# Listing each slot's token in PSUM instead of scattering rows to the experts

## The reference, cut to what matters

```python
x = x + gnn(xn, edge_index, ...) + mix(xn, ...)
...
logits = layernorm(x) @ gate_w + gate_b
probs = softmax(logits); idx = argmax(probs); prb = probs[idx]
pos = (cumsum(one_hot, axis=0) * one_hot).sum(-1) - 1     # place within the expert
kept = pos < C                                            # C = 1954
buf[idx, pos] = layernorm(x)                              # dropped where pos >= C
y = relu(buf @ w1[e] + b1[e]) @ w2[e] + b2[e]
x = x + y[idx, pos] * (prb * kept)
```

## Time and profile before

| what | us |
|---|---|
| median of 3 runs (lowest, highest) | 1644.87 (1641.97, 1651.89) |
| the profiled execution | 1646.12 |
| its span, first to last instruction | 1644.4 |
| PE busy in the span | 1414.5 |
| DVE busy | 1178.4 |
| ACT busy | 766.7 |
| POOL busy | 622.2 |

### The profile page before, as it was taken

The page is one execution under the profiler, slowest core; times in us unless marked ns, Lnnn a source line. Parts: engine busy times, 40 slices in busy tenths (PEclk is TensorE's granted clock), DMA queues, the critical chain, the costliest instruction groups (busy, mean ns, idle before and its releaser), DMA issues. The chain is left out here.

```text
span 1644.4 us, 29280 instructions
## 1 busy us (share of the span) xinstructions
PE 1414.5 (86%) x8633; PEld 1252.5 (76%) x8633; DVE 1178.4 (72%) x3066; ACT 766.7 (47%) x1455; POOL 622.2 (38%) x541
## 2 busy tenths in 40 slices
PE   6999999985858766777724999999999999999995
PEld 5999999974646555565524999999999999999995
DVE  5888888864777767777753676677767686767764
ACT  3455555531112111111114676766767676766762
POOL 1111111117787887888860122222122222222213
PEclk8999999996686787777766999999999999999998
DMA  3555555552445554555425212121121312131100
GB/s 108 127 122 120 119 122 130 127 161 59 105 106 123 125 114 107 113 119 121 104 67 127 76 40 72 44 77 47 41 87 50 94 42 77 48 100 50 26 14 18
DMA packets 122639, 145.22 MB, mean 88 GB/s; under 512 B 61546, under 2 KB 97390, under 8 KB 122469
## 3 DMA queue, kind: packets, MB, share of 16 engines
q1 hardware_dynamic: 70897, 89.24, 21.5%
q0 software_dynamic: 51696, 55.42, 14.0%
HBM read 76.42 MB, written 73.36 MB: 91 GB/s over the span
## 5 line engine op out<-in xcount | busy, mean ns | idle before, releaser
L1256 POOL DMA_INDIRECT out<-o_sb,tok_i x128 | 177.7, 1388 | 604.9 <-issue 604.9
L1454 DVE TENSOR_TENSOR h_lo<-hf,h_hi 128x496 fp32r<-128x496 f32 x256 | 172.8, 675 | 214.4 <-PE psY L1515 88.5
L1515 PE MATMUL psY<-w_hi,h_hi 128*124 128x256 f32 x1024 | 290.1, 283 | 7.6 <-DVE w_lo L1368 7.6
L1515 PE MATMUL psY<-w_hi,h_lo 128*124 128x256 f32 x1024 | 287.8, 281 | 0.0
L1515 PE MATMUL psY<-w_lo,h_hi 128*124 128x256 f32 x1024 | 287.2, 280 | 0.0
L1329 ACT ACTIVATE h_hi<-psH,b_sb 128x496 fp32r<-128x496 f32 x256 | 172.7, 674 | 230.0 <-PE psH L1538 219.5
L1515 PEld LDWEIGHTS psY<-w_hi,h_hi 128*124 128x124 f32 x1024 | 189.3, 185 | 16.0 <-issue 8.0
L1515 PEld LDWEIGHTS psY<-w_lo,h_hi 128*124 128x124 f32 x1024 | 189.5, 185 | 8.9
L1515 PEld LDWEIGHTS psY<-w_hi,h_lo 128*124 128x124 f32 x1024 | 189.7, 185 | 0.0
L1071 PE MATMUL psB<-inv_den,spread_at 128*128 128x125 f32 x400 | 84.0, 393 | 114.0 <-DVE inv_den L856 114.0
L1331 ACT ACTIVATE hf<-psH,b_sb 128x496 f32<-128x496 f32 x256 | 170.9, 668 | 0.0
(11 more groups left out here) (217 smaller groups left out, 3035.1 us busy)
## 6 DMA issues: line engine op xcount, KB each, us to landing
x_sb<-in_x SPq DMA_DIRECT2D x50, 448.0 KB
...
out<-o_sb,tok_i POOLq DMA_INDIRECT x128, 4.2
```

What stands on the lines that cost most here:

```text
L1256: pool.indirect_dma_start(out=out, in_=o_sb[:, par, j, :], in_offset=None, out_offset=bass.IndirectOffsetOnAxis(ap=tok_i[:, par, j:j + 1], ...
L1454: nc.vector.tensor_tensor(h_lo[:, f % 4, :], hf[:, f % 4, :], h_hi[:, f % 4, :].bitcast(F32), ALU.subtract).then_inc(s_hlo_ready, 1)
L1515: ins = nc.tensor.matmul(psY[par][j // 2][0:T3, (j % 2) * D:(j % 2 + 1) * D], hh[:, f % 4, j * T3:(j + 1) * T3], w[:, f, :], start=f == 0 ...
```

## The change

The buffer `expert_rows` goes, with the clears that fill it in stage 1, the row scatter of stage 2 and the loads of stage 3. Instead a list says which token each slot holds. A slot is written as a block and a row of it (slot = 124 block + row, NB = 128 blocks). DVE works out both in `place`; ACT makes, for each of a step's four tokens a partition, a one-hot of the row (124 wide) and one of the block (128 wide), the latter once with the token's index plus one and once with the probability's factor in place of the 1. It makes them by |i - row| and a Relu. PE multiplies the two (`listed`), and the sums of all 25 steps stay in one PSUM bank `psP`. After the last step DVE turns it into `row_at` (slots that stayed zero get an index out of bounds) and `prob`.

In stage 3 POOL gathers each tile's rows from the output, where stage 2 stored them, by four indirect DMAs with `row_at`, and scatters the results with it too. Empty slots are skipped by the gather, so DVE clears the four buffers first. The order on DVE changes: att_scores of step s+1 now stands ahead of `place(s)`. `positions` moves from a bank of its own to a part of `psD`, and `q_ksum` and `positions` get a wait for it.

```diff
-                def clear(g):
-                    pool.dma_start(groups[bass.ds(g, 1), :, :, :].rearrange("a p j w -> (a p) j w"),
-                                   empty[:, :].rearrange("p (a w) -> p a w", a=1).broadcast_to([P, J, RW]))\
-                        .then_inc(s_empty_out, 16)
...
                 pool.wait_ge(s_mhalf_set, 1)
-                for s in range(3):
+                rstd_of(0)
+                with pool.Fori(1, NS) as s:
                     rstd_of(s)
-                    clear(s)
-                with pool.Fori(3, NS) as s:
-                    rstd_of(s)
-                    clear(s)
-                with pool.Fori(NS, E * ROWS // (P * J)) as s:
-                    clear(s)
...
-                nc.gpsimd.iota(token[:, :], [[1, J]], base=0, channel_multiplier=J,
+                nc.gpsimd.iota(val[:, 0, :], [[1, J]], base=1 - TS, channel_multiplier=J,
                                allow_small_or_imprecise_dtypes=True)
-                nc.gpsimd.memset(xd[:, :, :, :], 0.0)
+                nc.gpsimd.iota(upto[:, 0:T3], [[1, T3]], base=0, channel_multiplier=0,
+                               allow_small_or_imprecise_dtypes=True)
+                nc.gpsimd.iota(upto[:, T3:T3 + NB], [[1, NB]], base=0, channel_multiplier=0,
+                               allow_small_or_imprecise_dtypes=True)
...
-                def scatter(s, par):
-                    pool.wait_ge(s_slots_ready, s + 1)
-                    passed(pool, s_pool_passed)
-                    for j in range(J):
-                        pool.indirect_dma_start(out=rows, in_=xd[:, par, j, :], in_offset=None,
-                                                out_offset=bass.IndirectOffsetOnAxis(ap=slots[:, par, j:j + 1], axis=0),
-                                                bounds_check=E * ROWS - 1, oob_is_err=False).then_inc(scat[par], 16)
...
                     if ahead == 2:
                         pool.wait_ge(s_pr, NPR * s + 1)
                         gather(s + 2, par, h + 2)
-                    scatter(s, par)
...
+                def one_hots(s):
+                    act.wait_ge(s_place, NPLACE * (s + 1))
+                    act.wait_ge(s_perm_mm, s)
+                    act.wait_ge(s_at_ready, 3 * J * s)
+                    act.activation(nval[:, :, :], val[:, :, :], ACT.Copy, scale=-1.0).then_inc(s_away, 1)
+                    passed(act, s_act_passed)
+                    for j in range(J):
+                        act.activation(away[:, j, 0:T3], upto[:, 0:T3], ACT.Abs, bias=row[:, j:j + 1], scale=-1.0)\
+                           .then_inc(s_away, 1)
+                    for j in range(J):
+                        act.activation(away[:, j, T3:T3 + NB], upto[:, T3:T3 + NB], ACT.Abs, bias=blk[:, j:j + 1],
+                                       scale=-1.0).then_inc(s_away, 1)
+                    act.wait_ge(s_away, NAWAY * (s + 1))
+                    passed(act, s_act_passed)
+                    for j in range(J):
+                        act.activation(at_row[:, j, :], away[:, j, 0:T3], ACT.Relu, bias=1.0, scale=-1.0)\
+                           .then_inc(s_at_ready, 1)
+                        for n in range(2):
+                            act.activation(at_block[:, j, n, :], away[:, j, T3:T3 + NB], ACT.Relu, bias=val[:, n, j:j + 1],
+                                           scale=nval[:, n, j:j + 1]).then_inc(s_at_ready, 1)
                 def step(s, par, h, ahead):
                     root(s)
                     logit_exp(s)
                     if ahead > 0:
                         att_exp(s + 1)
+                    one_hots(s)
...
-                    nc.vector.tensor_scalar(xd[:, par, :, D + 1], token[:, :], 0.0, None, ALU.add)
...
-                    nc.vector.tensor_scalar(token[:, :], token[:, :], float(TS), None, ALU.add)
...
-                def place(s, par):
+                def place(s):
                     dve.wait_ge(s_l_exp, s + 1)
                     nc.vector.tensor_reduce(lsum[:, :], lex[:, :, :], axis=AX.X, op=ALU.add).then_inc(s_route, 1)
                     dve.wait_ge(s_pos_mm, s + 1)
                     nc.vector.tensor_tensor(pos[:, :, :], cum[:, 0:J, :],
-                                            psC[0:T, 0:E].rearrange("p (a e) -> p a e", a=1).broadcast_to([T, J, E]),
+                                            psD[0:T, 128:128 + E].rearrange("p (a e) -> p a e", a=1).broadcast_to([T, J, E]),
                                             ALU.add).then_inc(s_route, 1)
                     nc.vector.tensor_tensor(seen[:, :], seen[:, :], cum[:, J, :], ALU.add)
                     dve.wait_ge(s_route, NROUTE * s + 9)
                     nc.vector.tensor_tensor(picked[:, :, :], pos[:, :, :], oh[:, :, :], ALU.mult).then_inc(s_route, 1)
-                    dve.wait_ge(s_route, NROUTE * s + 8)
-                    nc.vector.reciprocal(xd[:, par, :, D], lsum[:, :])
                     dve.wait_ge(s_route, NROUTE * s + 10)
                     nc.vector.tensor_reduce(slotf[:, :], picked[:, :, :], axis=AX.X, op=ALU.add).then_inc(s_route, 1)
+                    dve.wait_ge(s_at_ready, 3 * J * s)
+                    nc.vector.tensor_scalar(val[:, 0, :], val[:, 0, :], float(TS), None, ALU.add).then_inc(s_place, 1)
+                    dve.wait_ge(s_route, NROUTE * s + 8)
+                    nc.vector.reciprocal(val[:, 1, :], lsum[:, :]).then_inc(s_place, 1)
                     dve.wait_ge(s_route, NROUTE * s + 11)
-                    nc.vector.tensor_tensor(over[:, :], slotf[:, :], limit[:, :], ALU.is_ge).then_inc(s_route, 1)
-                    dve.wait_ge(s_route, NROUTE * s + 12)
-                    nc.vector.scalar_tensor_tensor(slots[:, par, :], over[:, :], BIG, slotf[:, :], ALU.mult, ALU.add)\
-                      .then_inc(s_slots_ready, 1)
+                    nc.vector.tensor_tensor(over[:, :], slotf[:, :], limit[:, :], ALU.is_ge).then_inc(s_place, 1)
+                    dve.wait_ge(s_place, NPLACE * s + 3)
+                    nc.vector.scalar_tensor_tensor(slotf[:, :], over[:, :], BIG, slotf[:, :], ALU.mult, ALU.add)\
+                      .then_inc(s_place, 1)
+                    dve.wait_ge(s_place, NPLACE * s + 4)
+                    nc.vector.tensor_scalar(blk[:, :], slotf[:, :], 1.0 / T3, 0.5 / T3 - 0.5, ALU.mult, ALU.add)\
+                      .then_inc(s_place, 1)
+                    dve.wait_ge(s_place, NPLACE * s + 5)
+                    nc.vector.tensor_scalar(blk[:, :], blk[:, :], ROUND, ROUND, ALU.add, ALU.subtract).then_inc(s_place, 1)
+                    dve.wait_ge(s_place, NPLACE * s + 6)
+                    nc.vector.scalar_tensor_tensor(row[:, :], blk[:, :], -float(T3), slotf[:, :], ALU.mult, ALU.add)\
+                      .then_inc(s_place, 1)
...
                         q_scaled(s + 1)
-                    place(s, par)
                     if ahead > 0:
                         att_scores(s + 1, 1 - par, h + par + 1)
+                    place(s)
+                    if ahead > 0:
                         att_sum(s + 1, 1 - par)
                         base_of(s + 1, 1 - par, h + par + 1)
...
+                dve.wait_ge(s_perm_mm, NS)
+                nc.vector.tensor_scalar(vacant[:, :], psP[0:T3, 0:NB], 0.0, BIG, ALU.is_equal, ALU.mult)\
+                  .then_inc(s_perm_set, 1)
+                nc.vector.tensor_copy(prob[:, :], psP[0:T3, NB:2 * NB])
+                dve.wait_ge(s_perm_set, 1)
+                nc.vector.scalar_tensor_tensor(row_at[:, :], psP[0:T3, 0:NB], -1.0, vacant[:, :], ALU.add, ALU.add)
...
                     pe.wait_ge(s_den_max, s)
+                    if not (isinstance(s, int) and s < 2):
+                        pe.wait_ge(s_route, NROUTE * (s - 2) + 9)
...
-                def positions(s):
+                def positions(s, ahead):
                     pe.wait_ge(s_cum_done, J * (s + 1))
                     pe.wait_ge(s_route, NROUTE * s)
-                    nc.tensor.matmul(psC[0:T, 0:E], before[0:T, :], cum[:, J, :], start=True, stop=False)
-                    nc.tensor.matmul(psC[0:T, 0:E], ones[0:T, :], seen[:, :], start=False, stop=True)\
+                    pe.wait_ge(s_den_max, s + 2 if ahead > 0 else NS)
+                    nc.tensor.matmul(psD[0:T, 128:128 + E], before[0:T, :], cum[:, J, :], start=True, stop=False)
+                    nc.tensor.matmul(psD[0:T, 128:128 + E], ones[0:T, :], seen[:, :], start=False, stop=True)\
                       .then_inc(s_pos_mm, 1)
+                def listed(s, last):
+                    pe.wait_ge(s_at_ready, 3 * J * (s + 1))
+                    for j in range(J):
+                        ins = nc.tensor.matmul(psP[0:T3, 0:2 * NB], at_row[:, j, :],
+                                               at_block[:, j, :, :].rearrange("p n b -> p (n b)"),
+                                               start=isinstance(s, int) and s == 0 and j == 0, stop=last and j == J - 1)
+                    ins.then_inc(s_perm_mm, 1)
```

(51 more changed lines are left out.)

73 lines of the change are left out of this document (38 added, 35 removed).

## The result

The changed kernel takes 1635.61 us (median of five runs, 1633.54 to 1636.45) against 1647.12 for the kernel before on the same chip: a ratio of 0.9927, 95% interval 0.9910 to 0.9943. The forecast was 1616, a gain of 29 us; 11.5 came.

The account below looks back on a forecast made before the run. POOL's indirect DMA issues were taken to set stage 2's step. Loop -31.3, last step -3.1, border +3.9, stage 3's start +3, stage 2's start -1.3: -28.8 against 1646.1, so 1616 as median; range 1595 (1593 with `b_bc` early) to 1644 us.

Parts of the forecast that it names:

- POOL's twelve issues: Stage 2: twelve indirect DMAs a step at 1.52 us, 18.2 us together, set the measured step of 18.46 us.
- DVE's new loop: Stage 2: DVE's own work, with the new place and att_scores moved ahead, gives a floor of 16.2 us a step.
- ACT's list: Stage 2: 21 added activations a step take 7.0 us, with bounds of 4.2 and 10.5.
- Rivals 1: Stage 2: ACT becomes the bound and the kernel slower; 1672 us at a list of 11 us; chance 7%.
- rival 3: Stage 2: PE is at the high clock all through, 16.2 us a step, 1595 us; chance 17%.
- So `gx` stops being last in nearly all steps: Stage 2: without scatters the gathered rows arrive by 26 to 31 us after place; DVE wants them near 31.
- rival 4: Stage 2: the index load or the landing holds `gx`, step as now, 1648 us; chance 4%.
- I take the slow pair in 60% of the steps, +0.9: Stage 2: list products and spread at PE's low clock delay DVE's q_scaled by 1.5 us, averaging +0.9 a step.
- 17.1: Stage 2: forecast step in us, down from 18.46, making the loop of 23 steps 31.3 us shorter.
- that covers the 5.5: Start of stage 3: DVE's 10.34 us stand for `b_bc` hides tile 0's rows coming 5.5 us later.
- The border: Last place to stage 3: list, its products, DVE's instructions and border take 14.8 us instead of 10.93, +3.9.
- Rival 5: Stage 2: an ACT table switch costs 1.38 us beyond its load, +0.6 us in 24 steps, 1632 us; chance 5%.

Follow-up runs that it names:

- e6: Kernel before, with the index and row loads of step s+2 issued ahead of the store of step s: 1645.72 us, ratio 0.9984.
- e1: Changed kernel, with the index and row loads of step s+2 issued ahead of the store of step s: 1600.23 us, ratio 0.9715.
- e11: e1 with 16 more activations a step at the head of ACT's list, written to an unread buffer: 1713.56 us, ratio 1.0403.
- e7: Kernel before, with the row scatters of each step and their waits left out: 1604.51 us, ratio 0.9720.
- e14: Kernel before without row scatters, loads of step s+2 ahead of the store, four unread PE products added a step: 1566.41 us, ratio 0.9502.
- e2: Changed kernel, with stage 3's broadcast of the second bias issued only after tile 0's gathered rows are in: 1626.86 us, ratio 0.9875.

## Why the prediction was wrong

**Right.** POOL's twelve issues set the step: the edit that gives 35 us after the change gave 2 before it (e6). DVE's new loop: forecast floor 16.2 us, measured 15.99 in e1. ACT's list: 7.0 forecast, 6.6 measured, and the root follows its load without a drain. The start of stage 2 and the last step are within 1.5 us. Rivals 1 and 3 are both nearer than their chances of 7% and 17%: ACT's slack at the floor is 0.5 us (e11), and PE did turn warm.

**First failed step: "So `gx` stops being last in nearly all steps".** It was last in 17 steps, 1.64 us a step. My sum had the gather "issued by 24 to 26 and in by 26 to 31", wanted "near 31", and took the middle of bounds whose late end met the limit exactly. Both landings were longer than I had them. In the step shown the index load's issue ends at 528.33 and the gather starts 6.5 us later, not 2 to 4.5 (median of all steps 5.3), and the last gather's rows are taken 6.3 us after its end (5.2 to 7.0), where the sum had 2 to 5. From the end of place, 519.87, that makes 27.1 for the last issue and 33.4 for the rows. The path place, store, index load, eight gathers, att_scores spans two steps and is the longer one. At their late end the rows that I had the earlier trace rows already gave no slack, and rival 4 ("the index load or the landing holds `gx`", 4%) had the mechanism, though not its size, since with POOL freed the wait shrinks from 2.4 to 1.64 us a step and doesn't stay.

**A second error in the same term, with the other sign.** "I take the slow pair in 60% of the steps, +0.9" did not come: DVE's wait for the spread is 4.9 us in all. The clock of the loop rose from 0.77 to 0.86, which rival 3 priced at 16.2 us a step and the forecast did not; e7, without the list, ran at 0.75, and e14 shows that added products can do it. Without the wait for `gx` the changed loop runs at (403.6 - 37.8) / 23 = 15.9 us. So 17.1 should have been 15.9 + 1.64. That the loop missed by only 10 us is luck: 38 us too few for `gx` and 28 too many for the rest.

**Second failed step: "that covers the 5.5".** Tile 0's late rows were to hide behind DVE's stand for `b_bc`, and +3 us was what the gathers would do to `b_bc`. I asked what the rows do to the broadcast and never what the broadcast does to the rows, though the earlier trace rows showed it on a quarter of the engines. Rows came 29.5 us after the first issue instead of some 10: e2 takes 16.5 of that away, and the term is +17.6. The last sign of being wrong that the prediction names, tile 0 behind `b_bc`, is what came. The rule cited there from the Trainium skill ("DMA: Bandwidth & Descriptors", SWDGE vs HWDGE vs iDMA), queues served in turn inside an engine, delays a gather as it delays a load; I applied it to the load alone. The runs agree that the two share (rows after 12.1 us beside neither, 13.0 beside the weights, 22.2 beside the broadcast, 29.5 beside both), and they don't tell taking turns from another kind of sharing.

**The border** was over-priced, +3.9 against +0.6: PE's list 3.77 and ACT's 6.6 us are as forecast, but DVE's three instructions take 0.7, not 1.0, and the border 0.55, not 2.79, the figure of the border before it. Rival 5's own terms, 0.6 us in 24 steps, give 1630 us and not 1632.
